# A state-space layer and a mixture of experts on one core: rows normalised in place, two output buffers, and the choice of two experts placed earlier

## The reference, cut to what matters

```python
x = layernorm(x + ssm(x))       # ssm: states by tanh(state @ A.T + x @ B.T), states @ C.T + D*x, own layernorm with gamma, beta
x = layernorm(x + ffn(x))
# ffn, per row: scores = sigmoid(x @ router.T); the better of two groups of four experts by its two best scores;
#   in it the two best experts, weights = their scores / their sum
#   routed = sum of two weighted experts  silu(x @ w_gate) * (x @ w_up) @ w_down ; plus one shared expert
```

## Time and profile before

| | |
|---|---|
| median of 3 runs | 401.82 us (398.14 to 402.32) |
| profiled execution, its own time | 399.13 us |
| its span, first to last instruction | 397.4 us |
| busy: PE, DVE, ACT, POOL | 314.7, 229.1, 186.1, 204.2 us |
| mean granted PE clock, share of full | 0.915 |
| passes with four tiles begin (L1117) at | 147.3, 181.2, 219.9, 257.4, 294.9, 326.4 us |

### The profile page before, as it was taken

One profiled execution on the slowest core, in us unless ns is written; L12 is line 12 of the kernel. 1 busy time (PEld: TensorE's weight loads), 2 busy tenths in 40 slices (PEclk: granted clock), 3 DMA queues, 4 the chain that ended last, 5 costly groups with the idle time before them and its releaser, 6 DMA issues.

```text
span 397.4 us, 7368 instructions
## 1 busy us (share of the span) xinstructions
PE 314.7 (79%) x2255; PEld 233.5 (59%) x2255; DVE 229.1 (58%) x671; ACT 186.1 (47%) x442; POOL 204.2 (51%) x326
## 2 busy tenths in 40 slices
PE   5999998866676498789939795969779879795960
PEld 5899887744465375457617363636446546584850
DVE  2346986328949819927990897099536615161430
ACT  1555225561753752853636264517644643453421
POOL 7895023314442782776395535635381555745632
PEclk9999999759999889969979998969898999998995
DMA  7990000000000000000001000100010010101000
GB/s 192 331 329 5 0 2 0 2 0 2 2 2 0 2 27 2 0 2 27 3 0 41 13 2 0 55 1 2 0 54 1 2 55 0 54 2 53 28 3 31
DMA packets 6811, 13.20 MB, mean 33 GB/s; under 512 B 1000, under 2 KB 3568, under 8 KB 6768
## 3 DMA queue, kind: packets, MB, share of 16 engines
q1 hardware_dynamic: 5232, 8.47, 6.8%
q0 software_dynamic: 1536, 4.20, 3.0%
HBM read 8.47 MB, written 4.19 MB: 32 GB/s over the span
## 4 chain that ended last, share of the span: by engine, by line
DVE 23%; PE 17%; issue 7%; POOL 7%; DMA 5%; ACT 3%; POOLq 0%; DVEq 0%; ACTq 0%
PE bank L454 7%; PE bank L431 7%; POOL out_dram L1358 5%; DMA out_dram<-wd,row_id 5%; DVE st L942 4%; DVE wg L1106 2%; DVE wu L1110 2%; ACT wd L750 1%; DVE ahead L1038 1%; DVE y L963 1%; DVE y L983 1%; DVE mv L946 1%; DVE score L1004 1%; DVE y L973 1%; DVE wu L1103 1%
## 5 line engine op out<-in xcount | busy, mean ns | idle before, releaser
L1314 POOL TENSOR_TENSOR h<-wu,h 128x512 f16<-128x512 f32 (+1 forms) x54 | 51.3, 951 | 74.6 <-ACT h L736 74.2
L431 PE MATMUL bank<-xT,wg 128*128 x324 | 67.3, 346 | 8.1 <-ACT comb_sorted L720 3.8
L454 PE MATMUL bank<-wd,h 128*128 (+1 forms) x504 | 72.7, 296 | 1.1 <-POOL h L1314 1.1
L727 ACT ACTIVATE wg<-bank,g_un 128x512 f32<-128x512 f32 (+1 forms) x54 | 32.0, 592 | 82.0 <-PE bank L431 52.9
L431 PE MATMUL bank<-xT,wu 128*128 x324 | 64.5, 336 | 0.0
L454 PEld LDWEIGHTS bank<-wd,h 128*128 128x128 f16 x504 | 51.6, 107 | 11.1 <-POOL h L1314 2.0
L1117 DVE CAST row_id<-bank 128x4 int32<-128x4 f32 (+1 forms) x10 | 1.6, 161 | 87.2 <-DMA out_dram<-wd,row_id 75.1
L431 PEld LDWEIGHTS bank<-xT,wg 128*128 (+1 forms) x324 | 31.8, 102 | 29.9 <-issue 13.1
L1358 POOL DMA_INDIRECT out_dram<-wd,row_id x32 | 32.6, 1019 | 32.1 <-ACT wd L750 25.2
L431 PEld LDWEIGHTS bank<-xT,wu 128*128 (+1 forms) x324 | 32.3, 100 | 23.9 <-issue 1.1
L1106 DVE SCALAR_TENSOR_TENSOR wg<-bank,u_un,wg 128x512 f32<-128x512 f32 (+1 forms) x44 | 27.3, 620 | 24.0 <-PE bank L431 14.9
(11 more groups left out here) (182 smaller groups left out, 568.3 us busy)
## 6 DMA issues: line engine op xcount, KB each, us to landing
xres<-in_L_attn_x_dram SPq DMA_DIRECT2D x7, 512.0 KB, 6.0
wd<-in_L_ffn_w_down_dram SPq DMA_DIRECT2D x1, 1024.0 KB, 6.8
xres<-in_L_attn_x_dram SPq DMA_DIRECT2D x2, 256.0 KB, 2.9
out_dram<-wd,row_id POOLq DMA_INDIRECT x32, 2.4
states<-in_L_attn_B_dram SPq DMA_DIRECT2D x1, 128.0 KB, 2.0
D_bc<-in_L_attn_D_dram SPq DMA_DIRECT2D x1, 128.0 KB, 5.1
beta_bc<-in_L_attn_beta_dram SPq DMA_DIRECT2D x1, 128.0 KB, 7.4
states<-in_L_attn_C_dram SPq DMA_DIRECT2D x1, 128.0 KB
```

The lines of the kernel that those rows point to most:

```text
L431: last = pe.matmul(ps[:, 0:w], up_rows[which][pw][:, part], x2_sorted[:, k * 2 + px, bass.ds(col, w)], start=first, stop=(k == KT - 1 and ...
L454: last = pe.matmul(ps_y[t // 2][:, (t % 2) * DM:(t % 2 + 1) * DM], h16[:, m % 3, ph, t * P:(t + 1) * P], down_rows[pw][:, rows], start=(fi ...
L727: nc.scalar.activation(sg[:, m % 2, 0:w], ps_g[:, 0:w], ACT.Silu, scale=g_un[:, 0:1]).then_inc(sems.silu_done, 1)
L1314: nc.gpsimd.tensor_tensor(h16[:, m % 3, 1, 0:w], h[:, m % 2, 0:w], h16[:, m % 3, 0, 0:w], ALU.subtract).then_inc(sems.h_low, 1)
```

## The change

It does five things. (1) `y1` is no buffer of its own any more: the rows are normalised in place in `xskip`, and small buffers per group grow from 2 to 3. `rows` no longer waits for the turned and split rows two groups back. (2) There are two buffers for the output rows (`z2s`), three places for `row_id`, and three semaphores for the sends. `note_rows` and `sums` of pass i and i - 1 now wait for sends of passes with the same place, the last of them pass i - 3. (3) `close` moves from j = 2 to j = 3, `deviations3` from j = 3 to j = 4, `finish` from j = 4 to j = 0 of the pass after it, and `send` from j = 4 to j = 0 and j = 1 of that pass, half of the tiles in each. (4) A third group (g = 2) goes through `project` to `sum_moments` in the first part; the first group's `permute` uses four banks of its own and its weights a fifth, so those copies wait for nothing, and `logits` and `scores` of group 1 come after them. (5) `choose_two` stands directly behind `sort_tiles` (j = 1), `weigh` in j = 2.

```diff
-        z2 = wd_flat[:, 0:T4 * DM].rearrange("p (t d) -> p t d", t=T4)
+        z2_even = wd_flat[:, 0:T4 * DM].rearrange("p (t d) -> p t d", t=T4)
-        y1 = sb("y1", [P, 2, T4, DM])
+        z2_odd = sb("z2_odd", [P, T4, DM])
+        z2s = [z2_even, z2_odd[:, :, :]]
+        def y1(g, par, sems):
+            return xskip[:, g * T4:(g + 1) * T4, :] if sems is main else again_rows[par]
+        def ps_rows(g, t):
+            return ps_misc[t % 2] if g else bank[t]
+        def ps_weights(g):
+            return ps_misc[0] if g else ps_y[0]
+        def sent_by(i):
+            return sum(TILES[k] for k in range(i % 3, i + 1, 3)) if i >= 0 else 0
...
# PE
                 for k in (1, 0):
                     if sems is main and k == 0 and g >= 2:
                         pe.wait_ge(main.comb_placed, g * 2 * T4)
+                        pe.wait_ge(main.y1_done, 2 * min(g + 1, G))
...
+                if i == 19:
+                    pe.wait_ge(main.y1_done, 4)
+                    project(2, 2 * T4, main)
                 if i == 27:
-                    pe.wait_ge(main.y1_done, 4)
+                    pe.wait_ge(main.y1_done, 6)
                     turn_x2(0, 0, main)
...
-            logits(1, main)
             for t in range(T4):
                 permute_main(0, t)
+            logits(1, main)
             turn_comb(0)
...
             up_main(0)
-            front_late(-1)
# ACT
+                if j == 0 and i >= 2:
+                    finish(i - 2, i % 2, TILES[i - 2], main)
                 if j == 1 and i:
-                    sums(TB[i - 1], TILES[i - 1], unit(i, 0), main)
+                    sums((i - 1) % 2, TILES[i - 1], (i - 3) % 3, sent_by(i - 3), unit(i, 0), main)
...
-                if j == 4 and i:
-                    finish(i - 1, TILES[i - 1], main)
# DVE
+            rows(2, 2, main)
+            scale_rows(2, 2, main)
+            sum_rows(2, 2, main)
+            sum_moments(2, 2, main)
             choose_group(0, main)
...
-                    note_rows(i, i % 2, TILES[i], TB[i - 1] if i else 0, main)
+                    note_rows(i, i % 3, TILES[i], i % 3, sent_by(i - 3), main)
...
                 g = due(n, EP - 1, 1)
                 if g is not None:
                     sort_tiles(g)
+                    choose_two(g, main)
...
-                if j == 2 and i:
-                    close(TB[i - 1], TILES[i - 1], main)
                 g = due(n, EP - 2, 1)
                 if g is not None:
-                    choose_two(g, main)
-                g = due(n, EP - 3, 1)
-                if g is not None:
                     weigh(g, main)
+                if j == 3 and i:
+                    close((i - 1) % 2, TB[i - 1], TILES[i - 1], main)
# POOL
-                if j == 3 and i:
-                    deviations3(i - 1, TB[i - 1], TILES[i - 1], main)
...
+                if j == 4 and i:
+                    deviations3(i - 1, (i - 1) % 2, TB[i - 1], TILES[i - 1], main)
...
-                if j == 4 and i:
-                    send(i - 1, (i - 1) % 2, TB[i - 1], TILES[i - 1], main)
+                if j in (0, 1) and i >= 2:
+                    half = TILES[i - 2] // 2
+                    send(i - 2, i % 2, (i - 2) % 3, TB[i - 2], TILES[i - 2], main, range(j * half, (j + 1) * half))
```

More of the change, by code:

```diff
@@ L352, in project @@
                 for half in range(2):
-                    if half and sems is main and g >= 2:
+                    if half and sems is main and g >= 3:
                         pe.wait_ge(main.th_done, g)
@@ L862, in _ @@
                             high(n, m, g * E + e - 1 if e else None, GT, again)
[L863 to L864 removed]
+                        sums(half, T4, 0, g * T4, (g + 1) * E1, again)
+                        finish(g, half, T4, again)
         @block.vector
@@ L1350, in plan_last, with send @@
                 nc.gpsimd.tensor_scalar(pass_i[0:1, NP, 0:1], taken[0:1, NP:NP + 1], -1.0, float(TB[NP] * P), ALU.mult, ALU.add).then_inc(pass_known, 1)
-            def send(i, par, before, tiles, sems):
+            def send(i, par, ring, before, tiles, sems, which=None):
                 pool.wait_ge(sems.ids_ready, i + 1)
-                for t in range(tiles):
+                for t in which or range(tiles):
                     pool.wait_ge(sems.out_ready, before + (t + 1))
@@ L1366, in _ @@
             deviations2(1, 1, main)
+            deviations1(2, 2, main)
+            deviations2(2, 2, main)
             plan(0)
@@ L1398, in _ @@
             low(NALL - 1, NALL - 1, TILES[NP] * P, main)
-            deviations3(NP, TB[NP], TILES[NP], main)
-            send(NP, NP % 2, TB[NP], TILES[NP], main)
-            pool.wait_ge(main.out_sent, 16 * L)
+            deviations3(NP, NP % 2, TB[NP], TILES[NP], main)
+            send(NP, NP % 2, NP % 3, TB[NP], TILES[NP], main)
+            for i in range(3):
+                pool.wait_ge(main.out_sent[(NP - i) % 3], 16 * sent_by(NP - i))
             pool.wait_ge(met_known, 1)
```

193 lines of the change are left out of this document (98 added, 95 removed).

## The result

The changed kernel took 367.32 us (median of 4 runs, 365.27 to 368.5) beside 400.02 of the kernel before: 0.9175 of its time, with a 95% interval of 0.9099 to 0.9251. The forecast was 364, its range 352 to 383. The profiled execution took 368.5, its span is 366.8, 30.6 less than before.

The account below looks back on a forecast made before the run. No engine was full: each pass was bound first by DVE, then by PE, plus a DMA wait. A 0, B -2.5, C -22.4 and D -10.5 sum to -35.4 from 399.13: 363.7, forecast 364, range 352 to 383.

Parts of the forecast that it names:

- C: Four full passes, from `choose_group` at 148.15 to that at 295.70: 147.55 becomes 4 x 31.3 = 125.2, so -22.4 us.
- D: The end, from 295.70: PE's waits for `row_id` (8.4) go, faster matmuls give about 2; -10.5 us.
- A: First part and pass 0: `choose_group` 3.9 us later, pass 0 gives some 3 back; net 0, bounds -3 and +4.
- B: Pass 1: 1.6 us of waiting before `choose_group` goes and a two-tile `close` (0.9) leaves its leg; -2.5 us.
- Leg 1: DVE-bound stretch of a four-tile pass, `choose_group` to end of `weigh`: 24.05 us less 1.71 of `close`, 22.35.
- R4: Rival: holds of DVE by POOL go, 1.8 us a pass; period 29.5, total 355; chance .07.
- Leg 2: Chain from the end of `weigh` to the end of the next `scores`, with DVE waiting for PE: kept at 8.9 us.
- (1), the ring: `row_id` places: sends of pass i - 3 issue about a period earlier, so `note_rows` meets no DMA; priced at nothing.
- (3), sends at nothing: Sends on POOL, now beside busy DVE with `low` queued behind: cost nil if a send costs the same there.
- R2: Rival: sends and DVE hold one another up, 1.0 us for each of 16 sends: +16, total 380; chance .12.
- R3: Slower rival: sends stall under DVE's first leg, `low` and `inner` wait; 16 sends cost 45 us, total 409; chance .03.
- R1: Rival: only the DMA wait goes, reordering brings nothing; period 32.95, total 370 (or 374); chance .19.

Follow-up runs that it names:

- choice_back: The changed kernel with its fifth part undone: `choose_two` in j = 2 and `weigh` in j = 3 again; 357.10 us, ratio 0.8948.
- no_sends: The changed kernel without the sends of passes 0 to 7 and their waits, most output rows unwritten; 368.15 us, ratio 0.9248.
- sends_late: The changed kernel with all sends of a pass in j = 4, two passes later; 403.11 us, ratio 1.0132.
- prologue_back: The changed kernel with the third group's `project` to `sum_moments` back in pass 0; 368.09 us, ratio 0.926.
- rings_only: The changed kernel with parts 3 and 5 undone, keeping buffers, semaphores and first part; 390.29 us, ratio 0.9751.
- comb_first: The changed kernel with `put_comb` ahead of `silu` and `high` on ACT; 370.59 us, ratio 0.9294.
- low_rows_later: choice_back with `low_rows` and `note_tiles` behind the first sends of a pass on POOL; 356.57 us, ratio 0.8898.
- two_mid: choice_back with `choose_two` behind `sum_rows`, ahead of the second routed `inner`; 364.96 us, ratio 0.9127.

## Why the prediction was right, and where not

The time (364 for 367) and each large term came out: C was -22.4 and is -22.0 (149.43 to 274.95 is 125.5 for the four passes), D was -10.5 and is -9.85 (101.7 to 91.85). A and B together were -2.5 and are +1.3 (149.43 against 148.15), which is 3.8 of the 4.8 us by which the profiled execution misses the sum. But C is right by two errors that cancel, and that is luck: a first leg 2.7 too long in the sum and a second leg 2.8 too short.

- **Leg 1, "22.35".** It has 19.68 on average, 21.16 in the pass shown. I took only `close` out of it; the third routed `inner` (1.44) leaves it too, since `weigh` now stands in front of it, which the order rows of the change show. Of the other 1.2 about 1.0 are holds beside POOL, 2.2 us a pass for 3.2 before: R4's term, in part.
- **Leg 2, "I keep 8.9".** It has 11.70. This is the step that failed. I measured leg 2 from the end of `weigh` as if PE and ACT would be ready then, and held that placing the two together "removes nothing by itself". It removes an `inner` from in front of `weigh`, and PE's `turn_comb` stands in its list behind the `spread` that needs this `inner`: 1.77 after `weigh` in place of 0.06, in every kernel with `weigh` in j = 2. `choose_two` in front of `scale_rows` to `sum_moments` makes `normalise` late, and `put_comb` behind it on ACT: 1.40 in place of 0.5. These 2.6 us are what parts 11.26, the second leg of the last two full passes, from choice_back's 8.64; the rest of the mean of 11.70 lies in the other two, mostly in the first (12.90). In choice_back (8.68) my leg 2 would have been right to 0.2.
- **A, "net 0", and B.** `choose_group` of the first group was later by 2.65 (3.9 expected) and the first `up` by 1.2 (3.2 expected). In the profiled execution passes 0 and 1 gave nothing back: the granted clock is 0.77 and 0.81, and rows on the path run at the lower level, such as the logits of pass 0 (16 matmuls in 3.56, 1.93 at full clock). That is one execution. By no_sends and sends_late, with the same lists there, A and B together are -3.8 and -4.0; and the total of prologue_back says net 0 for moving the group, as forecast. The miss of 3.8 is thus no more than executions of the same lists differ by, and the one profiled was the longest of the four.
- **(1), the ring.** Right that no DMA is waited for; sends_late shows that it is right only by the place of the sends.
- **(3), sends at nothing.** Right for the time, by no_sends: R2 and R3 fall. The 32 sends took 1.06 on average, the longest 1.43. But a send can last longer beside DVE, as R3 had it for all of them: in choice_back one takes 2.87 (rows below) and ends 0.9 after the `sum_rows` beside it, and sends of 2.39 to 2.98 stand beside `sum_rows` in five other runs, one or two in each. The first leg of that pass is the shortest of choice_back's four all the same (19.88). The Trainium skill's rule that I weighed (page "SBUF — State Buffer", section "SBUF: two separate sides": the descriptors of a DMA issued by GpSimd cannot be written while VectorE is in a 2-port operation) would have made 404 by my estimate. The time disagrees, and whether the operations beside the long sends are of that kind no run shows.

```profile
244.93 2.87 POOL L1382 DMA_INDIRECT out_dram<-z_odd,row_id  x1 [0.30 <-issue]
245.29 1.65 DVE L1002 SCALAR_TENSOR_TENSOR xskip<-xskip,rstd,xres 128x256 f32<-128x256 f32 x4
```

- **R1** (370, the reordering brings nothing) was right for neither piece of the reordering. Part 5 costs 10 us. Part 3, which the prediction priced at 1.7 a pass for `close` and nothing for the rest, carries some 32 of the 43 us that lie between the kernel before and choice_back. Why the sum missed this no run shows; my reading is that it measured from the kernel before, in which `close`, the sends and the wait share one stretch of time.

## What to carry to other kernels

A step that is moved ahead on one engine moves what it passes back: before asking what a moved step does for its own chain, ask which other engine waits for the rows that it now stands in front of, and read the end of the chain on every engine in it. Here `weigh` went in front of an `inner` (1.44), and its own successor on PE stands behind the `spread` that needs that `inner` (1.71). Ask, too, what the row will lie beside: a shifted list can cost as much by rows of DVE that POOL holds as by work. A forecast that comes out right as a sum is to be checked by its legs, and a change of five parts by undoing each: here one part gave most of the gain and another took a quarter of it back. And a clock read in one execution is to be checked in another of the same list before a cause is given for it. A wait for a buffer is cured by the place where the transfer is issued as much as by one more buffer.

## What was not expected of the hardware

A small DVE operation that reads SBUF can last to the end of the POOL operation beside it: `choice`, 128 x 32, 2.06 us to the end of `low_rows` (0.19 elsewhere). Summed over the rows from 75 us on that last at least 0.1 beyond the shortest of their line and shape, this is 12.4 us in the changed kernel, 10.8 in choice_back, 26.4 in rings_only and 24.6 in comb_first, so an edit on POOL or ACT can lengthen DVE's leg by shifting what lies beside what. DVE operations with an input in PSUM, such as `inner` at 218.32 in choice_back with `low` beside it from 218.89, kept their 0.75 and 0.69; in none of the fourteen traces does one last 0.1 longer than the shortest of its kind in that stretch.

The Trainium skill's page "SBUF — State Buffer", section "SBUF: two separate sides", states it as a lock: of a DVE operation in a 2-port mode or with two SBUF inputs and a GpSimd one, the first to start has the shared port for its whole length. The trace agrees in the row of 2.06, which starts 0.12 after `low_rows` in choice_back. `score`, which has one SBUF input and lasts 1.15 beside `low`, is held as well; in which mode it ran no run shows.

Five rows do not fit "the first to start". `mask` in rings_only (3.97) starts 0.68 before `low`, in the middle of a send, and lasts to the end of `low_rows` behind it. `top` in rings_only at 287.53 (5.18), `mask` in low_rows_later at 178.00 (2.96), `mask` in comb_first at 148.29 (2.15) and `level` in two_mid at 252.45 (1.97) start during a send, too, and outlast it to the end of a later operation on POOL. Other rows that start beside a send keep their 0.16 or 0.17, so what the send has to do with it stays open.
